# Row sums of the first attention: added up over the key tiles by VectorE, with one ones-matmul per head at the end of a block

## The chip, the cores and the metric

The kernel runs on one core of a Trainium2 chip. The metric is the device time in microseconds of one execution, as the median of a few. TensorE, VectorE (DVE in the rows), ScalarE (ACT), GpSimd (POOL) and SyncE (SP) each run their own list of instructions in order and wait for one another on semaphores.

## The reference, cut to what matters

Eight images of 256 channels and 1024 positions go through a group norm, a first attention without a mask (8 heads of 32), a residual, a layer norm, a second, causal attention, another residual, a layer norm and a mixture of experts. The part that the change touches is the softmax of the first attention:

```python
weight = jnp.einsum('bct,bcs->bts', q * scale, k * scale)
weight = jax.nn.softmax(weight.astype(jnp.float32), axis=-1)
a = jnp.einsum('bts,bcs->bct', weight, v).reshape(b, c, T)
```

The kernel computes exp(score - max) without dividing, multiplies it by the values, and divides at the end by the row sum of the exponentials. That row sum is what this change computes in another way.

## The kernel before

**Layout.** Channels lie on the 128 partitions. A group `g` is 4 heads (4 x 32 partitions), a half `hf` is 512 queries, a key tile `k` is 128 keys. A *block* is one (g, hf) of one attention; in the first attention (`st` = 0) it goes over all 8 key tiles. Each image has four such blocks, here called a, b, c, d, in the order (g0,h0), (g1,h0), (g0,h1), (g1,h1). Exponentials of one key tile are a `[128 keys, 4 heads, 512 queries]` fp32 tile of `probs`, which has two buffers.

**The step list.** `Steps.batch` writes out by hand the order of all work of an image as a list; every engine walks through the same list and emits its own share of each step, so the list is the order of work on every engine. There is no scheduler. A section "head" runs the first image without experts, the loop "body" runs seven times (experts of the image before, then both attentions of its own), "last" the experts of the last image.

**A mix step** `("mix", 0, g, hf, k, True)` on TensorE is: two scores of heads 0 and 1 into one buffer of `ps_two` (line 684), then the values product of the step before, `times_values(k-1)` (line 586, four heads side by side in 32 columns each), two scores of heads 2 and 3 into the other buffer, then `sums(k-1)` (line 595), which multiplies `probs` by `ones32` into `ps_acc[:, 1]`. The first step of a block has no values or sums. fp32 matmuls against `v_sb` and `ones32` are two instructions each in the rows, so a group for four heads is x8. ScalarE makes one exponential per score buffer (line 852, 128x1024).

**End of a block.** `norm` stands behind the first mix step of the next block: TensorE does `times_values` and `sums` of the last key tile, then ScalarE copies the values (`o_sb`, line 860) and VectorE the sums (`rsum`, line 1051), and both free `ps_acc` for the next block (`out_read`, `acc_read`). `div` (ScalarE lines 868, 870; VectorE 1056 to 1060) forms the quotient, `fin` (874, 1067) splits it into two parts for the matmuls of `out`.

**What else stands between the mix steps.** In b: norm, div, fin of a. In c: those of b, then `out(0,0)` (needs `fin`), `lna` (mean on TensorE line 712, subtraction on VectorE, squares on ScalarE line 883), `lnb` (variance on TensorE line 718, VectorE 1091, root on ScalarE 787/789, six operations on VectorE), `parts`. In d: the projections `qk` of the second attention, then the row maxima of its scores, `top` (TensorE 653/656 into `ps_two`, VectorE `reduce_max` line 1044) and `row` (666, ScalarE 834), four list entries behind each of d5, d6, d7 and two `v` steps. In a: nothing but `down(1)`, the last expert products of the image before, behind a0.

The list that is changed:

```python
a, b, c, d = (self.mix(0, g, hf, True) for hf in (0, 1) for g in (0, 1))
steps += a[:1] + ([("down", 1)] if experts else []) + a[1:] + b[:1] + [("norm", 0, 0, 0), b[1], ("div", 0, 0, 0), b[2], ("fin", 0, 0, 0)] + b[3:]
```

Of the kernel before, what the change touches and what calls it, by code (L numbers as in the profile page):

```python
# [8 lines left out]
ALU = mybir.AluOpType  # L9
# [6 lines left out]
HALF = 512  # L16
# [30 lines left out]
class Steps:  # L47
# [53 lines left out]
    def batch(self, experts):  # L101
        tops = rows_later(self.top(0, 0, 0) + self.top(0, 0, 1) + self.top(0, 1, 0) + self.top(0, 1, 1))
        if experts:
            steps = self.qk(0, 1, [0]) + [("logits",)] + self.v(0)[2:] + self.qk(0, 1, [1]) + [("inputs",)]
            steps += tops[:3] + [("turn",)] + tops[3:10] + self.experts_of(tops[10:])
        else:
            steps = self.v(0)[2:] + self.qk(0, 1) + tops

        a, b, c, d = (self.mix(0, g, hf, True) for hf in (0, 1) for g in (0, 1))
        steps += a[:1] + ([("down", 1)] if experts else []) + a[1:] + b[:1] + [("norm", 0, 0, 0), b[1], ("div", 0, 0, 0), b[2], ("fin", 0, 0, 0)] + b[3:]  # L110

        steps += c[:1] + [("norm", 0, 1, 0), c[1], ("div", 0, 1, 0), c[2], ("fin", 0, 1, 0), c[3]] + self.out(0, 0)
        steps += [c[4], ("lna", 0, 0), c[5], ("lnb", 0, 0), c[6], c[7], ("parts", 0)]
        steps += d[:1] + [("norm", 0, 0, 1), d[1]] + self.qk(1, 0, [0]) + [("div", 0, 0, 1), d[2], ("fin", 0, 0, 1)]
        t = rows_later(self.top(1, 0, 0))
        steps += d[3:5] + spread(d[5:8] + self.v(1)[:2], t)

        e, f, g, h = (self.mix(1, g, hf, hf == g) for hf in (0, 1) for g in (0, 1))
        t = rows_later(self.top(1, 1, 0))
        steps += e[:1] + [("norm", 0, 1, 1)] + self.qk(1, 1, [0]) + [("div", 0, 1, 1), e[1], e[2], ("fin", 0, 1, 1)]  # L120
        steps += [e[3]] + t[:3] + self.out(0, 1) + t[3:8] + [("lna", 0, 1)] + t[8:]
        steps += f[:1] + [("norm", 1, 0, 0), ("lnb", 0, 1), f[1], f[2], ("parts", 1), ("div", 1, 0, 0)]
# [19 lines left out]
N_CONSTS = 15  # L142


def events(steps):

    kinds = {}

    def add(kind, key):
        kinds.setdefault(kind, {})[key] = len(kinds.get(kind, {})) + 1  # L150

    turn = {"one": 0, "two": 0}

    def use(bank, key):
        add(f"{bank}{turn[bank] % 2}", key)
        turn[bank] += 1

    for s in steps:
        kind = s[0]
        add(kind, s)  # L160
        if kind in ("gn", "qk", "v", "out", "lna", "lnb", "logits", "turn", "up"):
            use("one", s)
        if kind == "mix":
            for n in range(2 if s[5] else HEADS_PER_GROUP):
                use("two" if s[5] else "one", s + (n,))
        if kind in ("top", "row"):
            use("two", s)
        if kind in ("norm", "down"):
            add("acc", s)
        if kind in ("split", "parts", "inputs"):  # L170
            add("acts", s)
        if kind == "stack":
            add(f"stacks{s[2]}{s[3]}", s[:3])
        for n in range(LINKS.get(kind, 0)):
            add("link", s + (n,))
    return kinds


def bass_hybrid_kernel(nc: bass.Bass, x, mats, vecs, norm_wb, sel_t, experts, out, w_dram):
# [8 lines left out]
    HD = P // G  # L188
# [51 lines left out]
    def last_tile(st, hf):  # L240
        return (PH * (hf + 1) if st else TT) - 1

    def last_mix(sec, s):

        _, st, g, hf = s
        return next(m for m in sec.no["mix"] if m[1:5] == (st, g, hf, last_tile(st, hf)))

    def half(hf):
        return slice(HALF * hf, HALF * hf + HALF)
# [1 line left out]
    with ExitStack() as ctx:  # L251
# [55 lines left out]
        gated_hi = nat[:, 2, :].rearrange("p (r t) -> p r t", r=2)  # L307
        gated_lo = nat[:, 3, :].rearrange("p (r t) -> p r t", r=2)
        gate_bc = probs[:, 1, :, :]

        ps_two = ctx.enter_context(nc.psum_tensor("ps_two", [P, 2, T], F32))
        ps_one = ctx.enter_context(nc.psum_tensor("ps_one", [P, 2, HALF], F32))
# [29 lines left out]
        v_ready = sem("v_ready")  # L342
        row_ready = sem("row_ready")
        mixed = sem("mixed")
        acc_read = sem("acc_read")
        out_read = sem("out_read")
        att_ready = sem("att_ready")
# [178 lines left out]
        def _(pe):  # L526
# [17 lines left out]
            def emit(sec, it):  # L544
# [22 lines left out]
                def times_values(s):  # L567
# [15 lines left out]
                            pe.wait_ge(out_read, sec.value("norm", sec.no["norm"][("norm", st, g, hf)] - 1))  # L583
                    for j in range(G):
                        c = P * g + HD * j
                        pe.matmul(ps_acc[HD * j:HD * j + HD, 0, a:HALF], v_sb[:, k, c:c + HD],  # L586
                                  probs[:, sec.no["mix"][s] % 2, j, a:HALF],
                                  start=(k == 0), stop=(k == last_tile(st, hf)))

                def sums(s):  # L590

                    _, st, g, hf, k, _ = s
                    a = first(st, hf, k)
                    for j in range(G):
                        mm = pe.matmul(ps_acc[HD * j:HD * j + HD, 1, a:HALF], ones32[:],  # L595
                                       probs[:, sec.no["mix"][s] % 2, j, a:HALF],
                                       start=(k == 0), stop=(k == last_tile(st, hf)))
                    mm.then_inc(mixed, 1)

                def times_down(hf, j):  # L600
# [12 lines left out]
                for s in sec.steps:  # L613
# [55 lines left out]
                    elif kind == "mix":  # L669
# [7 lines left out]
                        for n in range(G // per):  # L677
# [9 lines left out]
                                if diag:  # L687
                                    mm = pe.matmul(at[:, a:a + P], ident_bf[:], mask_kq[:], start=False, stop=True)  # L688
                            filled(mm, u)
                        if k > 0:  # L690
                            sums(("mix", st, g, hf, k - 1, wide))
                    elif kind == "norm":
                        _, st, g, hf = s
# [67 lines left out]
        def _(act):  # L761
# [6 lines left out]
            def emit(sec, it):  # L768
# [26 lines left out]
                    act.copy(keys_parts[:, m % 2, :], expert_sb[:, r, 0:C]).then_inc(keys_up, 1)  # L795

                gn_seen = lnb_seen = div_seen = 0
                for s in sec.steps:
                    kind = s[0]
                    if kind == "gn":  # L800
# [38 lines left out]
                    elif kind == "mix":  # L839
# [3 lines left out]

                        if sec.any("mix", n - 2):
                            act.wait_ge(mixed, sec.value("mix", n - 2))
                        if n <= 2 and sec.name == "body":

                            act.wait_ge(acc_read, sec.value("acc", sec.no["acc"][("down", NH - 1)]))
# [82 lines left out]
        def _(dve):  # L931
# [12 lines left out]
            def emit(sec, it):  # L944
# [32 lines left out]
                for s in sec.steps:  # L977
# [59 lines left out]
                    elif kind == "top":  # L1037
                        _, st, g, j, i = s
                        acc = full(s)
                        if i % PH == 0:  # L1040

                            if sec.any("row", sec.no["row"][("row", st, g, j, i // PH)] - G):
                                dve.wait_ge(row_ready, sec.value("row", sec.no["row"][("row", st, g, j, i // PH)] - G))
                        done(dve.reduce_max(tops[:, j, i:i + 1], acc[:, 0:cols(st, i)], AX_X), s)  # L1044
                    elif kind == "norm":
                        _, st, g, hf = s
                        dve.wait_ge(mixed, sec.value("mix", sec.no["mix"][last_mix(sec, s)]))
# [152 lines left out]
```

## Time and profile before

| | us |
|---|---|
| median of 3 runs | 4272.27 (4267.15 to 4276.54) |
| span of the profiled execution | 4288.4 |
| TensorE matmul busy | 3671.0 (86%) |
| VectorE busy | 2027.4 (47%) |
| ScalarE busy | 1710.8 (40%) |
| GpSimd busy | 771.3 (18%) |

The profiled execution is one run of its own; the profile gives its span, from the first to the last instruction, which lies 16 us (0.4%) above the median of the runs. Busy shares are means over stages with different limits. An image takes about 520 us, of which the four blocks of the first attention take about 143.

### The profile page before, as it was taken

To read this page: it belongs to the slowest core of one execution; us is meant where nothing else is said; L and a number is where in the kernel's file an instruction comes from. 1 tells how busy PE (TensorE), PEld (TensorE's weight loads), DVE (VectorE), ACT (ScalarE), POOL (GpSimd) and SP (SyncE) were. 2 spreads that over 40 slices of the span, in tenths; PEclk is the share of its full clock that TensorE was granted. 3 is DMA by queue.
4 is the path that set the end of the run, shared out by engine and by line. 5 is a ranking of instruction groups with operands and counts; after the bars stand their busy time and mean duration, and the time that the engine had idled before them with its cause. 6 is when DMAs were issued, how large, how long until landed. Compare 5 with 4: busy or idle time off the path is not lost.

```text
span 4288.4 us, 55007 instructions
## 1 busy us (share of the span) xinstructions
PE 3671.0 (86%) x18386; PEld 2033.9 (47%) x18386; DVE 2027.4 (47%) x2857; ACT 1710.8 (40%) x2732; POOL 771.3 (18%) x1051
## 2 busy tenths in 40 slices
PE   5898789987898878988889888898889987999867
PEld 3344563445634456344653445534464344644445
DVE  6334572355723566245652446424563345733533
ACT  1354335442354423634236342453334533354422
POOL 0000251002600035000430005300052001610035
PEclk7798899988998889989899798997898978999879
DMA  3011340114402143021420224202341113411134
GB/s 89 1 40 30 91 115 24 40 30 107 116 7 55 29 113 102 16 51 41 114 79 16 55 55 110 65 19 51 71 113 46 31 39 80 119 31 40 30 82 117
DMA packets 229749, 263.84 MB, mean 62 GB/s; under 512 B 137424, under 2 KB 139472, under 8 KB 229328
## 3 DMA queue, kind: packets, MB, share of 16 engines
q1 hardware_dynamic: 73808, 124.88, 12.1%
q0 software_dynamic: 155648, 135.17, 11.9%
q8 instruction: 170, 2.79, 0.3%
q14 instruction: 123, 1.01, 0.1%
HBM read 145.80 MB, written 9.44 MB: 36 GB/s over the span
## 4 chain that ended last, share of the span: by engine, by line
PE 57%; DVE 13%; DMA 11%; issue 8%; ACT 6%; POOL 2%; SPq 2%; DVEq 0%; ACTq 0%; POOLq 0%
PE ps_acc L586 9%; PE ps_two L684 9%; PE ps_acc L595 9%; DVE tops L1044 7%; DMA probs<-gates_dram 7%; PE ps_two L653 7%; PE ps_one L530 4%; DMA expert_sb<-experts_dram 3%; PE ps_one L531 3%; PE ps_one L532 3%; PE ps_one L684 3%; POOL nat L488 2%; SPq L414 1%; PE ps_one L718 1%; PE ps_one L725 1%
## 5 line engine op out<-in xcount | busy, mean ns | idle before, releaser
L1044 DVE TENSOR_REDUCE tops<-ps_two 128x1 bf16<-128x1024 f32 (+7 forms) x1024 | 983.4, 988 | 547.6 <-PE ps_two L656 401.1
L653 PE MATMUL ps_two<-stacks 96*128 96x512 f32 (+2 forms) x1792 | 664.5, 469 | 267.6 <-DVE tops L1044 198.6
L852 ACT ACTIVATE probs<-ps_two 128x1024 f32<-128x1024 f32 (+1 forms) x704 | 666.4, 963 | 385.0 <-PE ps_two L684 301.3
L476 POOL DMA_DIRECT2D expert_sb<-experts_dram x256 | 143.2, 561 | 2743.0 <-DVE rsum L1051 2608.9
L653 PEld LDWEIGHTS ps_two<-stacks 96*128 96x128 f32 x1792 | 355.8, 221 | 468.1 <-DVE tops L1044 270.9
L684 PE MATMUL ps_two<-stacks 97*128 97x512 f32 (+3 forms) x1408 | 525.4, 455 | 40.0 <-ACT probs L852 24.1
L684 PEld LDWEIGHTS ps_two<-stacks 97*128 97x128 f32 x1408 | 233.9, 195 | 523.7 <-issue 431.4
L586 PE MATMUL ps_acc<-probs,v_sb 128*32 128x512 f32 (+3 forms) x3584 | 466.8, 595 | 15.6 <-DVE rsum L1051 5.8
L595 PE MATMUL ps_acc<-probs,ones 128*32 128x512 f32 (+3 forms) x3584 | 452.2, 578 | 0.0
L488 POOL TENSOR_TENSOR nat<-expert_sb,nat 128x256 fp32r<-128x256 f32 x512 | 379.8, 746 | 369.8 <-ACT nat L795 271.3
L795 ACT CAST nat<-expert_sb 128x256 fp32r<-128x256 f32 x256 | 103.1, 406 | 831.5 <-DVE probs L1133 591.6
L1133 DVE SCALAR_TENSOR_TENSOR probs<-ps_one,probs 128x512 f32<-128x512 f32 x256 | 176.5, 689 | 320.2 <-issue 178.5
L1051 DVE COPY rsum<-ps_acc 128x512 f32<-128x512 f32 x64 | 44.2, 690 | 570.4 <-PE ps_acc L595 570.4
L834 ACT CAST stacks<-ps_two 1x512 fp32r<-1x512 f32 x256 | 148.2, 579 | 366.1 <-PE ps_two L666 361.8
L530 PE MATMUL ps_acc<-nat 128*128 128x512 f32 x512 | 221.7, 433 | 54.6 <-DVE nat L960 51.4
L852 ACT ACTIVATE probs<-ps_one 128x512 f32<-128x512 f32 (+3 forms) x384 | 170.1, 488 | 173.9 <-PE ps_one L688 99.7
L530 PE MATMUL ps_one<-act_hi,nat 128*128 128x512 f32 x512 | 222.3, 434 | 12.7 <-POOL nat L488 12.7
L530 PE MATMUL ps_one<-act_hi,w_hi 128*128 128x512 f32 x392 | 180.2, 460 | 45.2 <-DVE act_lo L1027 16.9
L532 PE MATMUL ps_one<-act_hi,nat 128*128 128x512 f32 x512 | 217.3, 424 | 0.0
L531 PE MATMUL ps_one<-act_lo,nat 128*128 128x512 f32 x512 | 217.3, 424 | 0.0
L481 POOL DMA_DIRECT2D probs<-gates_dram x256 | 209.3, 820 | 41.1 <-DMA gates_dram<-w_turn 17.4
L531 PE MATMUL ps_acc<-nat 128*128 128x512 f32 x512 | 213.6, 417 | 0.0
(128 smaller groups left out, 4721.8 us busy)
## 6 DMA issues: line engine op xcount, KB each, us to landing
stacks<-nat SPq DMA_DIRECT2D x792, 128.0 KB, 2.5
expert_sb<-experts_dram POOLq DMA_DIRECT2D x256, 256.0 KB, 5.2
probs<-gates_dram POOLq DMA_DIRECT2D x256, 256.0 KB, 8.6
x_in<-x_in_dram SPq DMA_DIRECT2D x9, 1024.0 KB, 4.9
out_dram<-x_res SPq DMA_DIRECT2D x16, 512.0 KB, 4.9
probs<-mats_dram SPq DMA_DIRECT2D x1, 2048.0 KB, 9.3
gates_dram<-w_turn SPq DMA_DIRECT2D x64, 16.0 KB, 1.5
sel_w<-sel_dram SPq DMA_DIRECT2D x1, 32.0 KB, 8.4
```

Source lines behind the costliest of these rows:

```text
L481: pool.dma_start(gate_bc[:, m % RING, :], bass.AP(row.tensor, row.offset, [[T, EPT], [0, H], [1, HALF]])).then_inc(gate_in[m % RING], 16)
L488: pool.tensor_tensor(parts[:, 2 + m % 2, :], expert_sb[:, m % RING, c:c + C], f(parts[:, m % 2, :]), ALU.subtract).then_inc(lowered, 1)
L530: pe.matmul(acc, lh, rh, start=start, stop=False)
L531: pe.matmul(acc, lh, rl, start=False, stop=False)
L532: return pe.matmul(acc, ll, rh, start=False, stop=stop)
L586: pe.matmul(ps_acc[HD * j:HD * j + HD, 0, a:HALF], v_sb[:, k, c:c + HD], probs[:, sec.no["mix"][s] % 2, j, a:HALF], start=(k == 0), stop=( ...
L595: mm = pe.matmul(ps_acc[HD * j:HD * j + HD, 1, a:HALF], ones32[:], probs[:, sec.no["mix"][s] % 2, j, a:HALF], start=(k == 0), stop=(k == l ...
L653: mm = pe.matmul(acc[:, c0:c1], q_st[0:MID, g, j, P * i:P * i + P], k_st[0:MID, g, j, c0:c1], start=True, stop=not diag)
L684: mm = pe.matmul(at[:, a:HALF], k_st[0:MID + 1, g, j, P * k:P * k + P], q_st[0:MID + 1, g, j, HALF * hf + a:HALF * hf + HALF], start=True, ...
L852: done(act.activation(probs[:, n % 2, per * i:per * i + per, a:HALF], acc[:, :, a:HALF], ACT.Exp, scale=SCALE), s + (i,))
L1044: done(dve.reduce_max(tops[:, j, i:i + 1], acc[:, 0:cols(st, i)], AX_X), s)
L1133: done(dve.scalar_tensor_tensor(out=gated[:, r, :], in0=acc, scalar=0.0, in1=gate_bc[:, r, :], op0=ALU.max, op1=ALU.mult), s)
```

## The change

For the first attention, VectorE now keeps `psums`, a `[128, 4, 512]` fp32 tile laid over `expert_sb` (free at that time): behind key tile 0 it copies the exponentials there, behind tiles 1 to 6 it adds theirs. TensorE leaves out `sums` for tiles 0 to 6 (the values product reports to `mixed` instead). At `norm` it does the ones-matmuls of tile 7 straight from `probs`, waits for the add of tile 6, and does four more ones-matmuls on `psums`, 512 columns each. ScalarE also waits, before the exponentials of a step, for the add of two steps before. VectorE's copy of tile 0 waits for the end of the block before (`mixed` of its last tile), since `psums` is one buffer. `down(1)` moves in front of a0, since `psums` shares `expert_sb`. The second attention is as before.

```diff
-        steps += a[:1] + ([("down", 1)] if experts else []) + a[1:] + b[:1] + ...
+        steps += ([("down", 1)] if experts else []) + a + b[:1] + ...
+def added_up(s):
+    return s[1] == 0 and s[4] < 7
...
+        psums = expert_sb[:, :, :]
...
                     for j in range(G):      # times_values
-                        pe.matmul(ps_acc[HD * j:HD * j + HD, 0, a:HALF], v_sb[:, k, c:c + HD],
+                        mm = pe.matmul(ps_acc[HD * j:HD * j + HD, 0, a:HALF], v_sb[:, k, c:c + HD],
...
+                    if added_up(s):
+                        mm.then_inc(mixed, 1)
...
                     for j in range(G):      # sums
                         mm = pe.matmul(ps_acc[HD * j:HD * j + HD, 1, a:HALF], ones32[:],
                                        probs[:, sec.no["mix"][s] % 2, j, a:HALF],
-                                       start=(k == 0), stop=(k == last_tile(st, hf)))
+                                       start=(k == 0 or st == 0), stop=last and st == 1)
+                    if st == 0:
+                        pe.wait_ge(added, sec.value("add", sec.no["add"][mix_at(sec, st, g, hf, k - 1)]))
+                        for j in range(G):
+                            mm = pe.matmul(ps_acc[HD * j:HD * j + HD, 1, :], ones32[:], psums[:, j, :],
+                                           start=False, stop=True)
...
-                        if k > 0:
+                        if k > 0 and not added_up(("mix", st, g, hf, k - 1, wide)):
                             sums(("mix", st, g, hf, k - 1, wide))
...
+                        if len(adds_seen) > 1 and sec.any("add", adds_seen[-2]):      # ScalarE, mix
+                            act.wait_ge(added, sec.value("add", adds_seen[-2]))
...
+                    elif kind == "mix" and added_up(s):      # VectorE
+                        for u in range(2 if wide else G):
+                            read(s + (u,))
+                        if k == 0:
+                            if sec.any("mix", sec.no["mix"][s] - 1):
+                                dve.wait_ge(mixed, sec.value("mix", sec.no["mix"][s] - 1))
+                            dve.tensor_copy(psums, probs[:, sec.no["mix"][s] % 2, :, :]).then_inc(added, 1)
+                        else:
+                            dve.wait_ge(added, sec.value("add", n - 1))
+                            dve.tensor_tensor(psums, psums, probs[:, sec.no["mix"][s] % 2, :, :], ALU.add).then_inc(added, 1)
```

## Rows read from the trace of the kernel before

**Rows 1.** The page's line of busy time per engine.

```profile
PE 3671.0 (86%) x18386; PEld 2033.9 (47%) x18386; DVE 2027.4 (47%) x2857; ACT 1710.8 (40%) x2732; POOL 771.3 (18%) x1051
```

**Rows 2.** Windows of blocks a, b, c, d: PE, PEld, DVE, ACT, POOL, clock.

```profile
1187.30:1224.10 36.80, 33.73 (x179) 11.17 (x178) 1.58 (x4) 18.73 (x20) 0.00 (x0) 0.91 0.04 15
1224.10:1250.60 26.50, 26.27 (x161) 7.45 (x162) 3.51 (x6) 18.50 (x21) 0.00 (x0) 1.00 0.01 2
1250.60:1283.60 33.00, 32.53 (x181) 11.22 (x181) 12.19 (x17) 21.14 (x24) 0.00 (x0) 1.00 0.00 0
1283.60:1330.00 46.40, 41.90 (x248) 17.92 (x248) 12.42 (x23) 23.26 (x28) 0.00 (x0) 0.96 0.16 35
```

**Rows 3.** Groups by form: the ones-matmuls of full width, both attentions.

```profile
L595 PE MATMUL ps_acc<-probs,ones 128*32 128x512 f32 x2816 | 387.4, 623 | 0.0
```

**Rows 4.** Timeline, block a, tiles 6 and 7: start, duration, instruction, wait.

```profile
1215.98 0.73 PE L684 MATMUL ps_two<-stacks 97*128 97x512 f32 x2
...
1218.31 1.06 PE L586 MATMUL ps_acc<-probs,v_sb 128*32 128x512 f32 x8
...
1219.30 0.73 PE L684 MATMUL ps_two<-stacks 97*128 97x512 f32 x2
...
1219.96 1.06 PE L595 MATMUL ps_acc<-probs,ones 128*32 128x512 f32 x8
1220.07 1.02 ACT L852 ACTIVATE probs<-ps_two 128x1024 f32<-128x1024 f32 x1 [0.64 <-PE ps_two L684]
```

**Rows 5.** Timeline, from the end of block a to tile 7 of b.

```profile
1224.08 0.69 DVE L1051 COPY rsum<-ps_acc 128x512 f32<-128x512 f32 x1 [31.20 <-PE ps_acc L595]
...
1224.90 1.07 PE L586 MATMUL ps_acc<-probs,v_sb 128*32 128x512 f32 x8 [0.23 <-DVE rsum L1051]
...
1245.81 0.73 PE L684 MATMUL ps_two<-stacks 97*128 97x512 f32 x2
```

**Rows 6.** Timeline, block c: TensorE waits for an exponential.

```profile
1275.79 2.88 ACT L852 ACTIVATE probs<-ps_two 128x1024 f32<-128x1024 f32 x3
...
1277.86 1.07 PE L586 MATMUL ps_acc<-probs,v_sb 128*32 128x512 f32 x8 [0.24 <-ACT probs L852]
```

**Rows 7.** VectorE on SBUF: two inputs at 1024 and 512, one at 512.

```profile
L1104 DVE TENSOR_TENSOR act_lo<-xn,act_hi 128x1024 fp32r<-128x1024 f32 x16 | 19.6, 1225 | 24.9 <-ACT act_hi L897 24.9
L1056 DVE TENSOR_TENSOR rsum<-rsum,rstd 128x512 f32<-128x512 f32 x64 | 44.2, 691 | 121.9 <-ACT rstd L870 121.9
...
L974 DVE TENSOR_SCALAR squares<-squares x32: 426/426/428, 242.0 to 4115.1; 128x512 f32<-128x512 f32 x32
```

**Rows 8.** Timeline, block c: lna, the root of lnb, tile 7.

```profile
1266.82 1.98 PE L712 MATMUL ps_one<-x_res,mean_w 128*128 128x512 f32 x4
...
1274.60 0.63 ACT L787 ACTIVATE rstd<-var_sb 128x512 f32<-128x512 f32 x1 [1.43 <-DVE var_sb L1091]
...
1278.86 0.74 PE L684 MATMUL ps_two<-stacks 97*128 97x512 f32 x2
```

**Rows 9.** Timeline, block d: tile 5, the first maxima, tile 6, later maxima.

```profile
1301.68 0.73 PE L684 MATMUL ps_two<-stacks 97*128 97x512 f32 x2
...
1303.86 0.62 DVE L1044 TENSOR_REDUCE tops<-ps_two 128x1 bf16<-128x128 f32 x2 [7.99 <-PE ps_two L656]
...
1305.38 0.73 PE L684 MATMUL ps_two<-stacks 97*128 97x512 f32 x2 [0.27 <-DVE tops L1044]
...
1313.95 0.49 PE L653 MATMUL ps_two<-stacks 96*128 96x512 f32 x1
```

**Rows 10.** Timeline around down(1): last row maximum, first exponential of a.

```profile
1187.03 0.38 PE L666 MATMUL ps_two<-minus_bf,tops 128*1 128x128 bf16 x4 [2.28 <-DVE tops L1044]
...
1192.99 2.87 ACT L852 ACTIVATE probs<-ps_two 128x1024 f32<-128x1024 f32 x3 [4.96 <-DVE x_res L1143]
```

**Rows 11.** Windows of 4 us in block a, columns as in Rows 2.

```profile
1192.00:1196.00 4.00, 1.39 (x10) 0.46 (x10) 0.87 (x2) 2.87 (x3) 0.00 (x0) 1.00 0.34 131
1196.00:1200.00 4.00, 4.00 (x16) 1.21 (x12) 0.00 (x0) 1.02 (x1) 0.00 (x0) 0.53 0.00 0
1200.00:1204.00 4.00, 4.00 (x20) 0.86 (x18) 0.00 (x0) 1.55 (x2) 0.00 (x0) 0.62 0.00 0
```

More of the change, by code:

```diff
@@ L109, in batch @@
         a, b, c, d = (self.mix(0, g, hf, True) for hf in (0, 1) for g in (0, 1))
-        steps += a[:1] + ([("down", 1)] if experts else []) + a[1:] + b[:1] + [("norm", 0, 0, 0), b[1], ("div", 0, 0, 0), b[2], ("fin", 0, 0, 0)] + b[3:]
+        steps += ([("down", 1)] if experts else []) + a + b[:1] + [("norm", 0, 0, 0), b[1], ("div", 0, 0, 0), b[2], ("fin", 0, 0, 0)] + b[3:]
         steps += c[:1] + [("norm", 0, 1, 0), c[1], ("div", 0, 1, 0), c[2], ("fin", 0, 1, 0), c[3]] + self.out(0, 0)
@@ L169, in events @@
             add("acc", s)
+        if kind == "mix" and added_up(s):
+            add("add", s)
         if kind in ("split", "parts", "inputs"):
@@ L241, in last_tile, with mix_at @@
         return (PH * (hf + 1) if st else TT) - 1
+    def mix_at(sec, st, g, hf, k):
+        return next(m for m in sec.no["mix"] if m[1:5] == (st, g, hf, k))
     def last_mix(sec, s):
         _, st, g, hf = s
-        return next(m for m in sec.no["mix"] if m[1:5] == (st, g, hf, last_tile(st, hf)))
+        return mix_at(sec, st, g, hf, last_tile(st, hf))
     def half(hf):
@@ L344, in bass_hybrid_kernel @@
         mixed = sem("mixed")
+        added = sem("added")
         acc_read = sem("acc_read")
@@ L585, in times_values @@
                         c = P * g + HD * j
-                        pe.matmul(ps_acc[HD * j:HD * j + HD, 0, a:HALF], v_sb[:, k, c:c + HD],
-                                  probs[:, sec.no["mix"][s] % 2, j, a:HALF],
-                                  start=(k == 0), stop=(k == last_tile(st, hf)))
+                        mm = pe.matmul(ps_acc[HD * j:HD * j + HD, 0, a:HALF], v_sb[:, k, c:c + HD],
+                                       probs[:, sec.no["mix"][s] % 2, j, a:HALF],
+                                       start=(k == 0), stop=(k == last_tile(st, hf)))
+                    if added_up(s):
+                        mm.then_inc(mixed, 1)
                 def sums(s):
@@ L593, in sums @@
                     a = first(st, hf, k)
+                    last = k == last_tile(st, hf)
                     for j in range(G):
@@ L596, in sums @@
                                        probs[:, sec.no["mix"][s] % 2, j, a:HALF],
-                                       start=(k == 0), stop=(k == last_tile(st, hf)))
+                                       start=(k == 0 or st == 0), stop=last and st == 1)
[4 more added lines that the diff above has]
+                                           start=False, stop=True)
                     mm.then_inc(mixed, 1)
@@ L797, in emit @@
                 gn_seen = lnb_seen = div_seen = 0
+                adds_seen = []
                 for s in sec.steps:
@@ L845, in emit @@
                             act.wait_ge(mixed, sec.value("mix", n - 2))
+                        if len(adds_seen) > 1 and sec.any("add", adds_seen[-2]):
+                            act.wait_ge(added, sec.value("add", adds_seen[-2]))
+                        adds_seen.append(sec.no["add"].get(s, adds_seen[-1] if adds_seen else 0))
                         if n <= 2 and sec.name == "body":
@@ L1044, in emit @@
                         done(dve.reduce_max(tops[:, j, i:i + 1], acc[:, 0:cols(st, i)], AX_X), s)
+                    elif kind == "mix" and added_up(s):
+                        _, st, g, hf, k, wide = s
+                        n = sec.no["add"][s]
+                        for u in range(2 if wide else G):
[7 more added lines that the diff above has]
+                            dve.tensor_tensor(psums, psums, probs[:, sec.no["mix"][s] % 2, :, :], ALU.add).then_inc(added, 1)
                     elif kind == "norm":
```

## The prediction, made before the changed kernel had run

> **What bounds the kernel now.** I read the page first: TensorE is busy 86% and VectorE 47% of the span [rows 1], so moving work from the one to the other looks free. The question is whether that holds where the change works. The windows of the four blocks of one image say: in b and c TensorE works without a gap (26.3 of 26.5 us, 32.5 of 33.0), at full clock, while ScalarE has 18 to 21 us and VectorE 3.5 and 12 us [rows 2]. So TensorE's list sets the pace there. The timeline shows one mix step as scores 0.66 us, values 1.00, scores 0.66, sums 1.00: from the second scores of tile 6 (1215.98) to those of tile 7 (1219.30) are 3.32 us [rows 4].
>
> **What is removed.** Seven of eight groups of ones-matmuls per block go, one group on `psums` comes: 6 groups of 1.00 us less, in 32 blocks (8 images by 4) 192 us of TensorE's time. (The rows count instructions: 2816 of full width for both attentions, 2048 of them in the first [rows 3].) That can be had only if TensorE stays the bound.
>
> **A steady step afterwards.** It doesn't. The values of a step need its second exponential. Second scores start at 0; their exponential starts at 0.77 (1219.30 to 1220.07 [rows 4]) and ends at 1.79; the values start 0.1 later (the second of three exponentials spaced 0.93 ends at 1277.74, the values start at 1277.86 [rows 6]); they take 1.00, and then the next second scores start. That loop is 2.88 us, though TensorE's own work is now only 2.32. Before, 0.44 us of slack hid it. A removed group is thus worth 0.44 us where nothing else stands between the steps, not 1.00.
>
> **What is added on VectorE.** A two-input operation takes 0.691 us at 512 and 1.225 at 1024 elements [rows 7], which extended by its slope gives 2.29 at 2048; with the gap behind it 2.33. A one-input operation from SBUF takes 0.426 at 512 [rows 7]; with a fixed part like the other's (0.157) it extends to 1.23 for the copy. The copy has no row of its own: 0.43, the row at a quarter of its size, bounds it from below, 2.29 from above; I take 1.25, from its nearest kind. The Trainium skill ("VectorE: DVE Perf Modes", the perf-mode tier table) gives an fp32 `tensor_copy` in SBUF two elements a cycle and 1227 ns at 2048; the sum would be the same, and no run so far shows it. Adds fit in 2.88 us when VectorE has nothing else. But VectorE's list is in order, and each add stands in front of the norm, div, fin, out, lna, lnb and top operations that TensorE and ScalarE wait for. So I walk through each block; time 0 is the start of the second scores of the last tile of the block before.
>
> **Boundary (b, c, d).** TensorE: first scores of the new block 0.66, the second need the buffer of the exponential that ends at 1.79, so 1.86 to 2.4; values of tile 7 to 3.4, sums to 4.4, the new group on `psums` to 5.4; `mixed` 5.5. VectorE was waiting for it with the copy in front of `rsum`: copy to 6.8, `rsum` (0.69 [rows 5]) to 7.5, first values of the new block at 7.6. Before they started at 5.60 (1219.30 to 1224.90 [rows 4, 5]). Cost 2.0 us, of which 1.3 is the copy.
>
> **Block b.** Second scores of tile 1 at 8.6, of tile 2 at 11.5. VectorE adds tile 1 from 10.4 to 12.7, so div (three of 0.72) runs to 14.9. ScalarE's `fin` waits for that and stands in front of the exponentials of tile 3, which come 1.2 late. Then 2.9 us a step: tile 7 at 27.3. Before: 26.51 (1219.30 to 1245.81 [rows 4, 5]). **+0.8.**
>
> **Block c.** The same to tile 3 (14.6). `out(0,0)` needs VectorE's `fin`, now behind the add of tile 2: 18.05, so TensorE stands 2.9 us. Its out groups run to 20.8; second scores of tile 4 at 22.4, lna from 23.1; VectorE's subtraction stands behind the add of tile 4 and is done at 28.0, the squares at 29.1, where lnb starts (TensorE stood 2.0). The variance is read behind the add of tile 5 (34.0), the logarithm starts at 34.1 and the root is done at 35.4, and ScalarE's exponentials of tile 6 stand behind it, so TensorE stands 3.1 more. Second scores of tile 7 at 38.3; VectorE's six operations of lnb (4.1 by [rows 7]) and the add of tile 6 end at 41.9, just in time. Before: 33.05 (1245.81 to 1278.86 [rows 5, 8]), with lna at 21.0 and the logarithm at 28.8 [rows 8]. **+5.2.**
>
> **Block d.** The boundary (+2.0), and the projections hide part of it; second scores of tile 5 at 23.3 against 22.8 (1278.86 to 1301.68 [rows 8, 9]). Then the maxima: the first of four stood 2.2 us behind those scores (1301.68 to 1303.86), now it waits for the exponential (1.79) and the add (2.33), 4.15. As each score buffer is freed by a maximum, the first scores of tile 6 come 5.8 us after instead of 3.7 (1305.38 [rows 9]). Tile 6 to tile 7: 7.2 (1.66 to its second scores, 1.79 + 2.33, then 1.42 as before) instead of 5.2; then 2.3 to the next maxima instead of 3.3, as tile 7 has no add. From tile 5 to there: 15.35 against 12.27 [rows 9]. Waits for the exponentials of tile 7 add 0.2, the group on `psums` in the norm behind e0 1.3 (1.0, more where the clock is low there). **+5.1.**
>
> **Block a.** Nothing stands between its steps, so it gains. With `down(1)` in front of a0, its matmuls no longer stand behind a0's four scores, and a0's exponentials had to wait for it anyway; on SP only its store is queued, which comes sooner. From the row matmul to the first exponential were 5.96 us (1187.03 to 1192.99 [rows 10]); without the scores in between, some 4.8. With 6 steps at 2.88 the second scores of tile 7 come at 1212.2 instead of 1219.3, less 2.1 given back if TensorE still runs at 1.2 GHz for a while, as the granted 0.53 and 0.62 show now: 3.4 us lost [rows 11], of which the new slack of 0.56 us in somewhat over two steps hides 1.3. **-5.0** in the loop; in the first image, without down, -3.0.
>
> **Other resources.** GpSimd and the DMA queues are idle in these blocks, the latter but for a share of 0.16 in d [rows 2], `expert_sb` is refilled only behind the second attention. These cost nothing.
>
> **Sum.** An image of the loop: -5.0 + 0.8 + 5.2 + 5.1 = +6.1; seven of them +43; the first +8.1: +51 us. To this comes the clock. The row of 1192 to 1196 has TensorE busy 1.39 of 4 us, and the next two have a granted clock of 0.53 and 0.62 with TensorE fully busy: (0.47 + 0.38) by 4 = 3.4 us lost [rows 11]. The new stops in c are 8 us in 23, and d has such at its maxima. I count one further such stretch per image at 3.0 us: +24. In all +75. Against the execution's own span, 4288 becomes 4363; on the median of the runs, 16 us lower, 4272 becomes 4347. The Trainium skill ("TensorE: Matmul & The Clock Gate", "A second HAM failure mode: psum-queue depth-cycling") says that short idle gaps between groups of matmuls alone can make the clock swing between half and full. The gap of 0.56 us in every steady step would be of that kind.
>
> **Rivals.**
> 1. *The clock falls oftener.* Three further stretches per image instead of one: +48 more, 4395. For it: the stops in c and d lie apart. Against: at 3.5 busy of 4 in d the clock was still full (0.96 over the block [rows 2]). If it fell through all steps, values and scores would take at most twice as long, a step 4.6 instead of 2.9, 28 steps an image: at most +394, about 4740. I give that 0.02, as the clock in b was 1.00 and in c, with its small stops, too [rows 2]. It is what the rule of the Trainium skill named above would come to here.
> 2. *The clock doesn't fall further*: 4323, or less where a keeps full clock throughout (-15): 4308.
> 3. *The copy at 2.29*: 1.05 more in three blocks of each image, +25: 4372.
> 4. *Faster: TensorE's list stays the bound.* If values needn't wait for the exponential of their own step, and the adds run in gaps as VectorE's 47% suggests, each removed group is worth 1.00. 192 less 31 for the copies: -161, 4111. It decides at c: the list gains if VectorE's `fin` is out before TensorE reaches `out`, that is if add plus fin take under 1.7 us behind the exponential. By [rows 7] they take 3.0. A part of this (my stops hidden half) would be about 4250. Together 0.11.
> 5. *Gains and stops cancel*: 0.04.
>
> **How the numbers follow.** Likeliest, the sum with one stretch, 0.40; rival 1 0.16 with its last case in it; rival 2 0.18; rival 3 0.11; faster 0.11; same 0.04. A change under 0.2% (about 9 us) can't be told from none in a measurement of this kernel. Slower 0.85, same 0.04, faster 0.11. The range 4285 to 4400 leaves out the faster cases below, the worst clock above; the likeliest case with its own bounds is 4325 to 4375.
>
> **What would show it.** In the profile after: line 595 with 1536 fewer records (24 matmuls of two instructions in each of 32 blocks), VectorE +15.0 us per block (1.25 + 6 x 2.29), in all about +480 us. Steps of a at 2.9 us. First values of b 7.6 us behind the second scores of a7. In c, `out` waiting for VectorE's act_lo, lnb for squares, exponentials behind the root; c about 38 us. In d, maxima 4.1 us behind the scores. It is wrong if steady steps take 2.3 us, if c is no longer than 33, or if the low clock covers whole blocks.

## The result, and the profile after

The changed kernel takes 4383.8 us (median of 4 runs, 4383.1 to 4385.7) against 4269.7 (4 runs, 4260.5 to 4276.5): a ratio of 1.0271, 95% interval 1.0254 to 1.0288. It is slower by 114 us. The forecast was 4347 (4285 to 4400). The profiled execution has a span of 4382.2 us, 94 more than the one before, whose own time lay above the runs' median; time per block is told below from these two executions.

Busy times from the page of the changed kernel, answering to [rows 1]:

```profile
PE 3524.7 (80%) x16850; PEld 2044.3 (47%) x16850; DVE 2491.0 (57%) x3081; ACT 1694.8 (39%) x2732; POOL 770.7 (18%) x1051
...
L1084 DVE TENSOR_TENSOR expert_sb<-expert_sb,probs 128x2048 f32<-128x2048 f32 x192 | 439.7, 2290 | 240.6 <-ACT probs L878 236.0
```

TensorE has 1536 matmul records fewer, as counted beforehand, but only 146 us less busy time, not 192; VectorE has 464 more. The windows of b, c and d (each from the end of VectorE's wait for `ps_acc` to the next such end; columns as in [rows 2]) of the image of [rows 2]:

```profile
1242.80:1271.30 28.50, 21.38 (x113) 7.52 (x113) 18.03 (x12) 17.66 (x20) 0.00 (x0) 0.94 0.00 1
1271.30:1313.30 42.00, 32.67 (x133) 12.18 (x134) 26.37 (x25) 20.99 (x25) 0.00 (x0) 0.84 0.00 0
1313.30:1371.80 58.50, 45.06 (x201) 22.71 (x202) 26.78 (x30) 23.05 (x28) 0.00 (x0) 0.77 0.12 27
```

The reader is to see that TensorE in c is busy as long as before (32.7 us against 32.5) although six of its groups are gone (seven left out, one added): the rest of its work ran at a granted clock of 0.84 instead of 1.00, in d at 0.77 instead of 0.96. A granted clock between 0.5 and 1 is a mean of the two levels, 1.2 and 2.4 GHz. Means over all eight images, from the start of one `rsum` copy to the next:

| us | before | after | forecast of the difference | measured |
|---|---|---|---|---|
| end of h to end of a (7 times) | 251.9 | 246.4 | -3.0 | -5.5 |
| b | 26.5 | 28.0 | +0.8 | +1.5 |
| c | 33.1 | 42.3 | +5.2 | +9.2 |
| d | 47.0 | 55.5 | +3.1 | +8.5 |
| e to h | 160.6 | 158.1 | 0 | -2.5 |

The prediction counts a, b and c to the second scores of their tile 7 and d to its `rsum` copy, so the boundary of 2.0 us behind a stands in its b, and here in a; its -5.0 for a is -3.0 here, and its +5.1 for d is +3.1. By the prediction's own marks the measured differences are -7.3 for a (forecast -5.0), +1.5 for b (+0.8), +6.8 for c (+5.2) and +12.7 for d (+5.1). The clock, forecast at +3 per image, isn't in the forecasts of the table.

**The steady step.** TensorE's timeline in block a (start, duration, instruction, idle time before it and what ended it), the tiles answering to [rows 4]:

```profile
1221.66 1.07 PE L599 MATMUL ps_acc<-probs,v_sb 128*32 128x512 f32 x8 [0.73 <-ACT probs L878]
1222.66 1.19 PE L705 MATMUL ps_two<-stacks 97*128 97x512 f32 x4
1224.60 1.06 PE L599 MATMUL ps_acc<-probs,v_sb 128*32 128x512 f32 x8 [0.74 <-ACT probs L878]
```

A step is 2.94 us (1221.66 to 1224.60), and the values product (L599) waits 0.73 to 0.75 us for the exponential in each. TensorE's own work in a step is 1.00 for the values and 1.20 for the joined scores, 2.20 us.

**The boundary.** Timeline at the end of block a, TensorE and VectorE, answering to [rows 5]:

```profile
1240.72 1.04 PE L611 MATMUL ps_acc<-probs,ones 128*32 128x512 f32 x8
1241.58 1.04 PE L617 MATMUL ps_acc<-expert_sb,ones 128*32 128x512 f32 x8
1242.55 0.73 PE L705 MATMUL ps_two<-stacks 97*128 97x512 f32 x2
...
1242.79 1.23 DVE L1081 COPY expert_sb<-probs 128x2048 f32<-128x2048 f32 x1 [4.12 <-PE ps_acc L617]
1243.93 0.68 DVE L1091 COPY rsum<-ps_acc 128x512 f32<-128x512 f32 x1
...
1244.74 1.06 PE L599 MATMUL ps_acc<-probs,v_sb 128*32 128x512 f32 x8 [1.46 <-DVE rsum L1091]
```

The copy of 1.23 us stands in front of `rsum`, and TensorE's first values wait 1.46 us for it, where it was 0.23.

**Block c.** Timeline, answering to [rows 6, 8]; first TensorE's three stops, then what VectorE did in front of the first two:

```profile
1283.59 0.50 PE L543 MATMUL ps_one<-act_hi,w_hi 128*128 128x512 f32 x1 [2.65 <-DVE act_lo L1107]
...
1294.78 3.00 PE L739 MATMUL ps_one<-squares,mean_w 128*128 128x512 f32 x4 [2.15 <-ACT squares L909]
...
1301.93 0.82 PE L705 MATMUL ps_two<-stacks 97*128 97x512 f32 x2 [1.43 <-ACT probs L878]
```

```profile
1280.51 2.28 DVE L1084 TENSOR_TENSOR expert_sb<-expert_sb,probs 128x2048 f32<-128x2048 f32 x1
1282.71 0.75 DVE L1107 SCALAR_TENSOR_TENSOR act_lo<-rsum,bias,act_hi 128x512 fp32r<-128x512 f32 x1
...
1290.03 2.29 DVE L1084 TENSOR_TENSOR expert_sb<-expert_sb,probs 128x2048 f32<-128x2048 f32 x1 [2.60 <-ACT probs L878]
1292.24 0.68 DVE L1126 TENSOR_TENSOR xn<-x_res,ps_one 128x512 f32<-128x512 f32 x1
```

Each time an add of 2.29 us stands in front of the operation that TensorE's next stop waits for (`fin` in L1107, lna's subtraction in L1126). The four lnb matmuls at 1294.78 then take 3.00 us, where four of the same shape (lna's, [rows 8]) took 1.98: the clock falls to 1.2 GHz while they run. Windows (columns as in [rows 2]) of two stretches of c:

```profile
1295.70:1299.00 3.30, 3.30 (x9) 1.20 (x11) 2.26 (x2) 0.85 (x1) 0.00 (x0) 0.50 0.00 0
1302.50:1312.60 10.10, 9.65 (x39) 2.89 (x38) 5.88 (x6) 5.11 (x6) 0.00 (x0) 0.50 0.01 2
```

What the clock does to a block can be read from the eight images of this one execution. In b it was 1.00 in three of them, with 27.2 us, and 0.94 in five, with 28.3 to 28.6. Here is c in the sixth and the seventh image:

```profile
2865.50:2909.40 43.90, 33.20 (x132) 13.67 (x132) 26.39 (x25) 20.93 (x25) 0.00 (x0) 0.81 0.00 0
3397.80:3437.50 39.70, 29.47 (x132) 12.16 (x132) 26.46 (x26) 21.31 (x25) 0.00 (x0) 0.91 0.00 0
```

With the same instructions, the image at 0.81 took 4.2 us more than the one at 0.91.

**Block d.** TensorE's timeline at the first maxima, answering to [rows 9]:

```profile
1330.56 0.73 PE L705 MATMUL ps_two<-stacks 97*128 97x512 f32 x2
...
1335.09 0.44 PE L674 MATMUL ps_two<-stacks 96*128 96x384 f32 x1 [2.23 <-DVE tops L1070]
...
1336.26 0.98 PE L705 MATMUL ps_two<-stacks 97*128 97x512 f32 x2 [0.26 <-DVE tops L1070]
1337.17 1.94 PE L599 MATMUL ps_acc<-probs,v_sb 128*32 128x512 f32 x8
```

From the scores of tile 5 to those of tile 6 are 5.70 us instead of 3.70, and after the stops of 2.2 us the clock falls: the values take 1.94 instead of 1.07.

### The profile page after: what moved, and what is told of

Read it like the earlier page. It is cut to its first block, busy times and chain, and to the rows that moved or that the text cites. A ratio compares the mean times of both kernels' runs of the same rounds, so it can differ in the third digit from the quotient of the medians.

```text
span 4382.2 us, 53160 instructions
## 1 busy us (share of the span) xinstructions
PE 3524.7 (80%) x16850; PEld 2044.3 (47%) x16850; DVE 2491.0 (57%) x3081; ACT 1694.8 (39%) x2732; POOL 770.7 (18%) x1051
## 3 DMA queue, kind: packets, MB, share of 16 engines
q14 instruction: 131, 1.07, 0.1%
## 4 chain that ended last, share of the span: by engine, by line
PE 47%; DVE 15%; issue 12%; ACT 11%; DMA 10%; POOL 2%; SPq 2%; DVEq 0%; ACTq 0%; POOLq 0%
PE ps_acc L599 8%; DVE tops L1070 7%; DMA probs<-gates_dram 7%; PE ps_two L674 6%; PE ps_two L705 6%; ACT probs L878 6%; PE ps_one L543 4%; PE ps_acc L611 4%; PE ps_one L544 4%; PE ps_one L545 3%; DMA expert_sb<-experts_dram 3%; PE ps_one L705 3%; POOL nat L501 2%; SPq L427 1%; PE ps_one L746 1%
## 5 line engine op out<-in xcount | busy, mean ns | idle before, releaser
L878 ACT ACTIVATE probs<-ps_two 128x1024 f32<-128x1024 f32 (+1 forms) x704 | 651.2, 962 | 414.2 <-PE ps_two L705 337.7
L599 PE MATMUL ps_acc<-probs,v_sb 128*32 128x512 f32 (+3 forms) x3584 | 491.0, 622 | 124.0 <-ACT probs L878 83.8
L1084 DVE TENSOR_TENSOR expert_sb<-expert_sb,probs 128x2048 f32<-128x2048 f32 x192 | 439.7, 2290 | 240.6 <-ACT probs L878 236.0
L705 PEld LDWEIGHTS ps_two<-stacks 97*128 97x128 f32 x1408 | 258.8, 208 | 484.5 <-issue 327.6
L611 PE MATMUL ps_acc<-probs,ones 128*32 128x512 f32 (+3 forms) x1792 | 211.0, 545 | 0.0
```

What stands on the lines that cost most here:

```text
L599: mm = pe.matmul(ps_acc[HD * j:HD * j + HD, 0, a:HALF], v_sb[:, k, c:c + HD], probs[:, sec.no["mix"][s] % 2, j, a:HALF], start=(k == 0), s ...
L705: mm = pe.matmul(at[:, a:HALF], k_st[0:MID + 1, g, j, P * k:P * k + P], q_st[0:MID + 1, g, j, HALF * hf + a:HALF * hf + HALF], start=True, ...
L878: done(act.activation(probs[:, n % 2, per * i:per * i + per, a:HALF], acc[:, :, a:HALF], ACT.Exp, scale=SCALE), s + (i,))
L1084: dve.tensor_tensor(psums, psums, probs[:, sec.no["mix"][s] % 2, :, :], ALU.add).then_inc(added, 1)
```

## The experiments

Times are medians; ratios are to the kernel before, timed on the same occasion (its median lay between 4268.0 and 4277.6), with 95% intervals. Times per block are means over the images of one execution, from `rsum` copy to `rsum` copy.

**1. The copy behind norm.** VectorE emits the copy of tile 0 just before the next mix step, so behind norm:

```diff
+                    if kind == "mix":
+                        add_up()          # emits what is held
...
+                    elif kind == "mix" and added_up(s) and s[4] == 0:
+                        held[:] = [s]
```

> The copy of tile 0 into psums is emitted on VectorE behind norm instead of in front of it; all else as in the changed kernel. Theory (VectorE's list order): TensorE's first values of b, c and d start 1.15 us sooner (the rsum copy no longer stands behind the 1.23 us copy), 3 x 8 x 1.15 = 28 us less, 4356. Rival (the boundary is set by TensorE's own groups or by ScalarE): no change, 4384.

Measured: 4374.2 (4354.6 to 4393.8), ratio 1.0251 (1.0206 to 1.0295). At the boundary the first values came 0.96 us behind the scores before them, where they came 2.19 behind (1242.55 to 1244.74 above), so the 1.2 us were gained in place:

```profile
1232.93 0.73 PE L705 MATMUL ps_two<-stacks 97*128 97x512 f32 x2
1233.89 1.06 PE L599 MATMUL ps_acc<-probs,v_sb 128*32 128x512 f32 x8 [0.23 <-DVE rsum L1113]
```

The total can't be told from the changed kernel's (the intervals overlap), and its median does not reach 4356. Block b was 26.0 us long where the granted clock was 1.00, and 33.1 where it was 0.69, against 27.2 to 28.6 at 0.94 to 1.00 in the changed kernel: what the boundary gave, the clock partly took. The place is shown, its price in the total is not.

**2. Every add later.** All adds stand just before the next mix step on VectorE:

```diff
-                    elif kind == "mix" and added_up(s):
-                        ...
+                    elif kind == "mix":
+                        add_up()
+                        held[:] = [s] if added_up(s) else []
```

> Each add (and the copy) is emitted on VectorE just before the next mix step, behind whatever stands between the two steps. Same adds, same number, same sizes. Theory (the loss is that norm, div, fin, out, lna, lnb and the maxima stand behind a 2.3 us add): the stops go, c falls from 42.0 to 32 or less, d from 58.5 to about 45, clock in c and d back at 0.95 or more; total 4200. Rival (VectorE's added 490 us of work costs by itself, wherever it stands): c and d stay above 38 and 52, total 4330 or more.

Measured: 4329.0, ratio 1.0138 (1.0121 to 1.0155); c 38.3 and d 54.1 us. Half of the loss went, and 4200 was far off; total, c and d are what the rival said. Its reason, that the added work costs by itself, doesn't follow, as a new wait came in place of the old. ScalarE's timeline in c:

```profile
1270.55 1.94 ACT L878 ACTIVATE probs<-ps_two 128x1024 f32<-128x1024 f32 x2 [1.56 <-DVE expert_sb L1018]
...
1292.82 1.94 ACT L878 ACTIVATE probs<-ps_two 128x1024 f32<-128x1024 f32 x2 [4.69 <-DVE expert_sb L1018]
```

`probs` has two buffers, and an add that is let behind VectorE's chain of lnb frees its buffer late. Over the execution ScalarE waited 90.0 us for adds, 49 times; in the changed kernel it was 1.0 us, 2 times. Between these two places of the adds, VectorE's order chose who waited.

**3. TensorE keeps its ones-matmuls** (what they sum is thrown away), while VectorE adds:

```diff
-                    if added_up(s):
-                        mm.then_inc(mixed, 1)
...
-                                       start=(k == 0 or st == 0), stop=last and st == 1)
-                    if st == 0:
+                                       start=(k == 0 or (st == 0 and last)), stop=...)
+                    if st == 0 and last:
...
-                        if k > 0 and not added_up(...):
+                        if k > 0:
```

> TensorE keeps all its ones-matmuls of tiles 0 to 6 (their sums are thrown away when tile 7 starts the accumulation anew), while VectorE adds as in the changed kernel. Theory (a good part of the loss in c and d is the low clock, which comes with TensorE's idle time): c 38.7 and d 53.5 us at a granted clock of 0.95 or more, so that the total is about 4390, no more than the changed kernel's, although TensorE does 168 more groups of 1.0 us. Rival (the clock's share is small, the stops alone are the loss): the kept groups come on top where steps are not bound by the exponential, 4440 or more.

Measured: 4393.4, ratio 1.0296 (1.0275 to 1.0317). Its windows of b, c, d:

```profile
1244.60:1273.20 28.60, 27.11 (x169) 7.65 (x169) 18.05 (x12) 18.40 (x20) 0.00 (x0) 1.00 0.00 1
1273.20:1313.10 39.90, 35.27 (x193) 11.88 (x190) 26.37 (x25) 21.11 (x25) 0.00 (x0) 0.96 0.00 1
1313.10:1368.30 55.20, 45.56 (x257) 19.07 (x258) 26.79 (x31) 23.27 (x29) 0.00 (x0) 0.91 0.13 29
```

The seven groups per block are back, and the total is 10 us longer (the intervals overlap), not 224 (the expectation says 168 groups; there are 7 in each of 32 blocks, 224). On the mean c takes 39.9 us (forecast 38.7) and d 55.1 (53.5), both no longer than without the groups (42.3 and 55.5); b is 0.6 us longer and the stretch to the end of a 2.1. The granted clock, 0.84 in c and 0.79 in d on the mean of the changed kernel, is 0.95 and 0.87 here: higher, but in d below the 0.95 expected. So what the change takes from TensorE in c and d is worth nothing there. What VectorE holds up sets most of their length, and the time freed is lost again to a lower clock.

**4. Short adds.** Only 128 of the 512 queries are added for tiles 1 to 6:

```diff
-   dve.tensor_tensor(psums, psums, probs[:, ..., :, :], ALU.add)
+   dve.tensor_tensor(psums[:, :, 0:P], psums[:, :, 0:P], probs[:, ..., :, 0:P], ALU.add)
```

> The adds of tiles 1 to 6 cover 128 of 512 queries (0.69 instead of 2.29 us), the copy of tile 0 and TensorE's work are unchanged; row sums are incomplete for the other queries. Theory (length of the add in VectorE's queue): steps of a stay at 2.93 us (the exponential sets them), c falls to about 34, d to about 47, with the clock near 1.0; total 4220. Rival (missing TensorE work lowers the clock whatever the adds take): clock in c and d stays at 0.85 or less, total 4320 or more.

Measured: 4268.0, ratio 0.9998 (0.9985 to 1.0011). b 26.0, c 35.0, d 50.6 us on the mean; the granted clock is 0.90 in c (0.86 to 0.95 by image) and 0.82 in d (0.77 to 0.83). The length of the adds is worth 116 us, as much as the whole loss. That it is no faster than before leaves a second part: c and d are still 1.9 and 3.6 us longer than before, which eats what a and b gain. What stays there are the copy of 1.23 us, the short adds of 0.69 and the lower clock; how much each of them takes wasn't tried. Of both expectations one half came: the time fell, but the clock stayed low.

**5 and 6. Adds in block a alone, and down(1) alone moved.**

```diff
+BLOCKS = [(0, 0)]
-    return s[1] == 0 and s[4] < 7
+    return s[1] == 0 and (s[2], s[3]) in BLOCKS and s[4] < 7
```

> Only block a (the first of the four of an image, with nothing between its mix steps) adds up on VectorE; b, c and d keep their ones-matmuls as before the change. down(1) stands in front of a0 as in the changed kernel. Theory (the add is free where VectorE has nothing behind it, each removed group is worth the 0.4 us that the exponential leaves): a 4.4 us shorter per image, b, c, d 26.5, 33.0 and 47 us as before, 4235 to 4230. Rival (the low clock follows the missing TensorE work even there, or the group on psums eats the gain): 4268 or more.

> The kernel before with only down(1) moved in front of a0. Theory: 1.1 us less in each of seven images, 4260. Rival (the scores in front only filled a wait): 4268.

Measured: 4249.7, ratio 0.9951 (0.9936 to 0.9966), and 4245.8, ratio 0.9948 (0.9928 to 0.9969). Moving `down(1)` alone gives 23 us, more than my 8. Its own part is as forecast: from the row matmul to the first exponential are 4.79 us, where it was 5.96 in [rows 10]:

```profile
1172.70 0.38 PE L666 MATMUL ps_two<-minus_bf,tops 128*1 128x128 bf16 x4 [2.16 <-DVE tops L1044]
...
1177.49 2.87 ACT L852 ACTIVATE probs<-ps_two 128x1024 f32<-128x1024 f32 x3 [3.79 <-DVE x_res L1143]
```

The rest came together with a higher clock: over the last 27 us of a it was 0.89 to 0.93 in every image before, and with `down(1)` first 1.00 in five images and 0.91 to 0.93 in three. The adds in a on top give nothing that can be measured, although b and c were exactly as before; 5 stayed behind its 4235. From `down(1)` to the end of a it took 29.5 us in five of seven images without adds and 32 in two; with adds 27.7 to 29.1 in four, but 31.8, 33.2 and 37.2 in three. Windows of 5 for a short one and the longest:

```profile
1183.00:1210.70 27.70, 20.45 (x117) 7.78 (x116) 16.26 (x9) 17.41 (x18) 0.00 (x0) 1.00 0.05 20
1694.90:1732.10 37.20, 33.02 (x117) 11.58 (x116) 16.24 (x10) 17.47 (x19) 0.00 (x0) 0.59 0.04 15
```

The instructions are the same, and TensorE's took 33.0 us instead of 20.5 at the lower clock. Why the clock fell in some images and not in others isn't shown.

**7 and 8. Both score pairs before the values.** In block a with its adds alone, and in all four with late adds:

```diff
-                            if n == G // per // 2 and k > 0:
+                            if n == G // per // 2 and k > 0 and not (st == 0 and (g, hf) in BLOCKS):
                                 times_values(("mix", st, g, hf, k - 1, wide))
...
                             filled(mm, u)
+                        if k > 0 and st == 0 and (g, hf) in BLOCKS:
+                            times_values(("mix", st, g, hf, k - 1, wide))
```

> As the one with only block a, and in block a TensorE emits both score pairs of a step before the values of the step before, so that those values no longer wait for an exponential that is just running. Theory (a steady step of 2.93 us is set by the loop second scores, exponential, values): the step falls to about 2.35 us, TensorE's own work (VectorE's add of 2.33 is then just as long), 7 steps by 0.55 by 8 images = 30 us less than the one with only block a, about 4200. Rival (ScalarE's or VectorE's rate sets the step): no change against it.

> Late adds in all four blocks, and both score pairs before the values. In the late-adds run ScalarE's exponentials of c and d waited for the add of two steps before (6 us in one c), as there are two buffers of exponentials. Theory (the exponential loop sets the plain steps, the two buffers the rest): a and b 3 to 4 us shorter each, c and d little changed, 4329 less 8 x 7 = 4270. Rival (the two buffers set the pace everywhere, since an add frees a buffer later than TensorE did): 4320 or more.

Measured: 4187.5, ratio 0.9812 (0.9797 to 0.9826), and 4190.7, ratio 0.9816 (0.9800 to 0.9831). TensorE's timeline in a of the first:

```profile
678.71 1.41 PE L707 MATMUL ps_two<-stacks 97*128 97x512 f32 x4
680.05 1.07 PE L600 MATMUL ps_acc<-probs,v_sb 128*32 128x512 f32 x8
681.05 1.39 PE L707 MATMUL ps_two<-stacks 97*128 97x512 f32 x4
```

The step fell to 2.34 us, and the values no longer wait. Now VectorE's adds set the pace: they run without a gap (11.60 us for five, 2.32 each), and the exponentials wait 0.39 us for them in a step. In 5 and in 7 TensorE goes from scores to values and back once in a step, so no such change is saved here, only the wait, and that settles what the 2.94 us were. It gave 62 us, twice the 30 expected: from `down(1)` to the end of a it now takes 22.8 to 24.2 us in every image, at a granted clock of 0.92 to 1.00, and the images with 31.8 to 37.2 are gone. In 8, against late adds in the old order, b fell from 28.6 to 24.5, c from 38.3 to 36.6 and d from 54.1 to 46.1; the total came out 80 us below the expectation, which had c and d little changed.

**9, 10 and 11. The order taken apart from the adds.** Adds late in a and b alone with the order; the changed kernel with the order; the kernel before with the order:

```diff
# the kernel before, 11
-                            if n == G // per // 2 and k > 0:
+                            if n == G // per // 2 and k > 0 and st == 1:
                                 times_values(("mix", st, g, hf, k - 1, wide))
...
                             filled(mm, u)
+                        if k > 0 and st == 0:
+                            times_values(("mix", st, g, hf, k - 1, wide))
```

> Blocks a and b add up on VectorE, with each add just before the next mix step, and both score pairs before the values in a and b; c and d as before the change. Theory: b was 24.4 us with this order where it was 26.5 before, and c and d are left alone (33.0 and 46.5), so 8 x 2.1 = 17 us less than with block a alone, about 4172. Rival (what b gains c gives back at the boundary, by the group on psums): 4187.

> The changed kernel (adds in all four blocks at their first place) with both score pairs before the values. Theory: plain steps go from 2.93 to about 2.35, a and b gain 3 to 4 us each, while the stops of c and d, which wait for VectorE, stay (c above 38, d above 50): 4384 less 8 x 8 = 4320. Rival (the wait for the exponential is most of the loss everywhere): 4268 or less.

> The kernel before with both score pairs before the values, in the first attention, and nothing else changed. Theory (before the change TensorE's own 3.32 us set the step, and the exponential had 0.4 us of slack): 4268, no change. Rival (the order is worth something by itself, so that the gain of the kernels with both isn't due to the adds): 4240 or less.

Measured: 4186.2, ratio 0.9797 (0.9767 to 0.9827); 4235.0, ratio 0.9917 (0.9884 to 0.9950); 4175.9, ratio 0.9771 (0.9742 to 0.9800). The last was a plain miss of mine. The order alone, without a single add, gives 2.3%. Experiment 10 came out below both of its numbers, with c at 37.5 and d at 51.5 us: the stops of c and d stand, but the order gave more than the plain steps of a and b. 9 has the rival's total and not its reason: c was 33.1 as before, b 2.6 us shorter than in 7, and d (47.4 against 46.5) and the stages behind it took that back. TensorE's timeline of 11 in b:

```profile
1194.67 1.20 PE L684 MATMUL ps_two<-stacks 97*128 97x512 f32 x4
1195.80 1.07 PE L586 MATMUL ps_acc<-probs,v_sb 128*32 128x512 f32 x8
1196.68 1.04 PE L595 MATMUL ps_acc<-probs,ones 128*32 128x512 f32 x8
1197.65 1.20 PE L684 MATMUL ps_two<-stacks 97*128 97x512 f32 x4
```

A step is 2.98 us instead of 3.32 with the same matmuls: four scores take 1.13 instead of twice 0.66, values and sums together 1.85 instead of 1.99. I had taken 3.32 for TensorE's own time; 0.34 of it belonged to the two more changes a step between the full-width scores and the 32-column groups. Against this base the adds of the changed kernel cost 59 us (4235.0 to 4175.9): c takes 37.5 us instead of 30.8 and d 51.5 instead of 45.1, while b takes 22.5 instead of 23.8. With late adds (9) b gains nothing (23.96 us).

**12. Both gains.** Adds in a alone, `down(1)` first, the order in all four blocks.

> Adds on VectorE in block a only, down(1) first, both score pairs before the values in all four blocks. In the kernel before with that order b, c, d took 23.8, 30.8 and 45.1 us; in the kernel with adds and that order in a alone, down(1) to the end of a took 23.4 where the former took 28.4. Theory (both gains add up): 8 x 5 us less than 4176, 4138. Rival (a's gain is lost to the clock or to the stage behind): 4170 to 4190.

Measured: 4134.9 (4127.4 to 4139.9), ratio 0.9689 (0.9668 to 0.9710), the fastest of all. b, c, d take 23.8, 30.8 and 45.0 us, the end of h to the end of a 240.7 (with the order alone 247.9). How much of those 7 us the adds give and how much `down(1)` wasn't taken apart with the new order.

## Why the prediction was right

**Sign and mechanisms.** Slower was forecast at 0.85, and the time lies inside the range. The stops stood where they were put. First values of b: 7.4 us behind the second scores of a7 (1237.33, the start of the joined scores, to 1244.74), forecast 7.6. Copy 1.23 and add 2.29 us, as taken. Steady step 2.94, forecast 2.88 (TensorE stands 0.74 of it; the prediction had 0.56, as it took its work for 2.32 where it was 2.20). In c `out` waited 2.65 us for act_lo (forecast 2.9), lnb 2.15 for the squares (2.0), the scores of tile 7 for an exponential (1.43; 3.1 forecast, but part of it was filled by work at the lower clock). Scores of tile 5 to 6 in d: 5.70, forecast 5.8. Experiments 2 and 4 moved or shortened the adds, with the same groups gone from TensorE, and took 55 and 116 us off, so the adds' place and length are the cause of the loss; 7 took the wait for the exponential away and with it the bound of the steady step.

**The term that was mis-sized** is the clock: "I count one further such stretch per image at 3.0 us". In the image shown, (1 - 0.84) x 42.0 + (1 - 0.77) x 58.5 + (1 - 0.94) x 28.5 = 21.9 us of TensorE's time at full clock were lost in b to d, idle time counted too, where it was 1.9 before. It fell to the lower level six times in them, against once. Of this the work shows most: less six groups of 1.00 us, TensorE's busy time in b, c and d should have fallen to 20.3, 26.5 and 35.9 us and was 21.4, 32.7 and 45.1, 16 us more. By the prediction's marks b, c and d came out 21.0 us longer together, and its stops alone gave 11.1. The difference of some 10 us an image, where 3 were counted, is a subtraction and no measurement of the clock alone; that c took 4.2 us more at 0.81 than at 0.91 shows its kind and size. c was to take about 38 us and took 39.8 by those marks (42.3 from copy to copy). Rival 1 had three stretches an image, 9 us; the total of 4384 stands close to its 4395. Its last case didn't come: between the low stretches the clock was full again, and over the last 27 us of a it was 0.81 to 1.00, with 1.00 in four of eight images, in spite of a stop in every step. Experiment 3 shows the sign of it: groups put back, clock up, c shorter by 2.4 us. How much each block owes to the clock alone can't be read from it, as the groups themselves take time.

**Luck in the total.** Against the executions' 94 us the forecast had 75. The clock's excess of some 7 us an image was hidden, for more than half, by two gains that its sum didn't have: a gained 7.3 us instead of 5.0, and e to h, where the change touches nothing, took 2.5 less. The length of e to h goes with the granted clock: 158.6 to 159.4 us at 0.86 to 0.87 and 161.6 to 161.9 at 0.84 in the images of before and of experiment 6, and 156.7 to 157.5 at 0.88 to 0.89 in six images of the changed kernel. Why it fell less there wasn't tried.

**The down(1) move** was right in its 1.1 us and missed the clock that went with it: 23 us alone (experiment 6) instead of 8.

**A wrong belief that didn't touch the forecast,** but two expectations: that TensorE's step before was all its own work. The trace of before held the sign of it: at the boundary of a and b, four scores side by side take 1.13 us where elsewhere a pair takes 0.66:

```profile
1220.96 1.20 PE L684 MATMUL ps_two<-stacks 97*128 97x512 f32 x4
1222.09 1.06 PE L586 MATMUL ps_acc<-probs,v_sb 128*32 128x512 f32 x8
```

## What to carry to other kernels

An idle engine is only free where nothing that others wait for stands behind the new work in its list: count what is queued behind each new instruction, and how long a buffer is held that the old reader gave back sooner. Work taken from the busiest engine is worth its time only until the next loop (here scores, exponential, values) sets the pace, and the gaps that it leaves can cost the clock. Before moving work off an engine, order what it has: matmuls of one shape put side by side made this kernel 2.3% faster, where the move made it 2.7% slower.

## What the runs showed of the hardware

Changes between full-width matmuls (97 rows by 128 columns) and groups of four in 32 columns cost about 0.17 us each: 3.32 to 2.98 us a step with two fewer. The Trainium skill says that this is so ("TensorEngine Tiling (Array Packing)", Key Properties: changing the tiling mode drains TensorE); the runs agree in kind and add the price.

The granted clock fell in blocks where TensorE was busy most of the time but with stops of 1.4 to 2.7 us between (c: busy 32.7 of 42.0 us, clock 0.84). In the image shown it kept 1.00 in the last 27 us of a, with a stop of 0.74 in every step, at nearly the same busy share:

```profile
1216.90:1243.90 27.00, 20.18 (x114) 7.56 (x114) 16.10 (x8) 18.06 (x20) 0.00 (x0) 1.00 0.06 20
```

In other images of the same execution it was down to 0.81 over that stretch, with the same instructions. In experiment 3, with c busy 35.3 of 39.9 us, it was 0.96. What decides between these isn't shown.
